# Two cross-attention layers on one core: ScalarE drains a slot's first unit ahead of the exponential and the copy of the maxima

## The chip, the cores and the metric

The kernel runs on one core of a Trainium2 chip. TensorE multiplies matrices into PSUM, ScalarE (ACT) and VectorE (DVE) work on PSUM and SBUF, GpSimd (POOL) works on SBUF and issues DMAs, SyncE (SP) issues DMAs. The metric is the device time of one execution in microseconds; of several executions the median is given.

## What is computed

For each of 16 batch entries a query matrix `x` of 112 rows and 320 columns passes through two cross-attention layers over the same context of 375 rows and 192 columns. Layer 0 has 8 heads of 40 columns over 371 context rows, and a second, small attention path over the last 4 rows, whose result is added before the output projection. Layer 1 has 20 heads of 16 columns over all 375 rows. Cut to what matters:

```python
# layer 0
hs = mha(x @ Wq, enc @ Wk, enc @ Wv)            # 8 heads, 371 keys
ca_hs1 = mha(ca_q1, x, x)                       # 112 x 112 scores for each head
ca_hs2 = mha(ca_hs1 @ Wq, ca @ Wk_ca, ca @ Wv_ca)   # 4 keys
x1 = (hs + ca_hs2) @ Wout + b_out + x
# layer 1
q, k, v = x1 @ Wq, ctx @ Wk, ctx @ Wv           # 20 heads, 375 keys
out = softmax(q k^T / 4) v @ Wo + bo + x1
```

## The kernel before

**Groups and slots.** The attention of both layers runs in groups of four heads: two groups of layer 0 and five of layer 1 for each batch entry. The main loop has 18 iterations (`t` from 0 to 17, `ITERATIONS`) of seven slots (`SLOTS`); each slot works on three groups at once, one in each stage:

- *scores*: TensorE computes the scores of a group in two halves into `bankS` (`scores`, L1120 for layer 0, L1124 for layer 1), and VectorE takes the row maxima of each half (L762);
- one slot later, *maxima*: TensorE transposes the maxima into `bankO` (`transpose_m`, L1137), VectorE copies them to `mT` (L768), and ScalarE issues a small DMA that places them as an additional row of the queries (`place_m`, L569 for layer 0, L572 for layer 1);
- two slots later (`LAG`), the *late* group: TensorE computes the transposed scores with the maxima already subtracted into `bankST` (`shifted_scores`, L1153 and L1166; this waits for the placed maxima), ScalarE takes the exponential (`exps`, L557 and L558 for layer 0, L561 for layer 1), and TensorE multiplies it with the values into `bankO` (`attend`, L1200; this waits for the exponential). VectorE copies the product (L779).

**Units.** All the rest (projections, transposes, the small attention path) is cut into 35 units for each batch entry. Each fills one of two PSUM banks (`bankX`), which alternate in the order of the units; a unit may be written only when the unit two before it is drained. The table `UNITS` gives for each slot two lists, phase 0 and phase 1, as names and offsets of the batch entry against `t`:

```python
([("W2", 1), ("V1_0", -1)], [("q1T_0", -1), ("V1_1", -1), ("q1T_1", -1)]),
([("V1_2", -1), ("q1T_2", -1), ("K1_0", 0)], [("N1a", -2), ("q0", 1), ("p3T", 0)]),
([("K1_1", 0), ("N1b", -2), ("S2_0", 1)], [("hn1T", -2), ("K1_2", 0), ("S2_1", 1)]),
([("K0_0", 1), ("q0T_0", 1)], [("K0_1", 1), ("out1", -2)]),
([("N0", 0), ("K0_2", 1), ("q0T_1", 1)], [("hn0T", 0), ("T2_0", 1), ("V0_0", 1)]),
([("T2_1", 1), ("out0", 0), ("V0_1", 1)], [("x1T", 0), ("PV2", 1)]),
([("q1", 0), ("S3", 1)], [("V0_2", 1)]),
```

`units_of(t, i, phase)` leaves out those whose batch entry doesn't exist, so in the first and last iterations a list may begin with another unit or be empty. K0, K1, V0, V1, q0, q1, out0 and out1 are projections (L968), five to nine matmuls each in split precision; q0T, q1T, hn0T, hn1T, x1T, T2, N0, N1a and N1b are transposes; W2, S2, PV2, S3 and p3T belong to the small path.

**The order on each engine** is written out by hand, and each engine works its program in order. TensorE in a slot: first half of the scores, transposed scores of the late group, transpose of the maxima, units of phase 0, second half of the scores, attend of the late group, units of phase 1. VectorE: maximum of the first half, copy of the transposed maxima, phase 0, maximum of the second half, copy of the attended product, phase 1. ScalarE, in the loop that the diff touches (L697 to L707): exponential of the late group, DMA of the maxima, phase 0, phase 1.

**Drains.** `unit` of ScalarE copies a filled bank to SBUF: K1 at L603, K0 at L609, V0 at L616, V1 at L624, q0 at L632, q1 at L637, q0T at L642, q1T at L648, W2 at L653, T2 at L655. For N0, N1a, N1b, out0 and out1 it returns at once, since VectorE alone drains these. For K0, K1, q0, q1 and W2 ScalarE writes the rounded part, and VectorE subtracts it afterwards to get the rest (L798 for K1, L803 for K0, L753 for q0, q1 and W2); only then is the bank free. S2 is drained by four exponentials (L579), after VectorE's maximum (L820).

Of the kernel before, what the change touches and what calls it, by code (L numbers as in the profile page):

```python
# [57 lines left out]
def units_of(t, i, phase):  # L58

    return [(name, t + off) for name, off in UNITS[i][phase]  # L60
            if 0 <= t + off < B and not (off == 1 and t < 0)]
# [30 lines left out]
def scored_at(t, i, before=0):  # L92

    n = SLOTS * t + i - before
    return SCORED.get((n // SLOTS, n % SLOTS))
# [22 lines left out]
def xattn_kernel(nc, xT, xpad, ctxT, caS, caT, w_all, w_ca, wqT, bd96, consts, bias, out):  # L118
    g_rows = nc.dram_tensor("g_rows", [B, 3, 32, HID], F32, kind="Internal").ap()

    with ExitStack() as ctx:
# [414 lines left out]
        def _(act):  # L536
# [12 lines left out]
            def exps(g):  # L549
                layer, b, k = g  # L550
                n = NUMBER[g]
                dst = PT[:, n % 2]
                act.wait_ge(st_done, n + 1)
                if n >= 2:
                    act.wait_ge(pv_done, n - 1)
                if layer == 0:
                    nc.scalar.activation(dst[0:KC, 0:2, :], bankST[0:KC, 0:2, 0:GROUP * SQ], ACT.Exp)  # L557
                    nc.scalar.activation(dst[0:KC - NTOK, 2, :], bankST[0:KC - NTOK, 2, 0:GROUP * SQ], ACT.Exp)\  # L558
                        .then_inc(exp_done, 1)
                else:  # L560
                    nc.scalar.activation(dst[0:KC], bankST[0:KC, :, 0:GROUP * SQ], ACT.Exp).then_inc(exp_done, 1)  # L561

            def place_m(g):
                layer, b, k = g
                n = NUMBER[g]
                src = mT[:, n % MT_BUFS, :].bitcast(F32)
                act.wait_ge(mT_copied, n + 1)
                if layer == 0:
                    act.dma_start(q0T[M_ROW0:M_ROW0 + 1, GROUP * k:GROUP * k + GROUP, :].bitcast(F32),  # L569
                                 src.unsqueeze(1)).then_inc(m0_placed, 16)  # L570
                else:
                    act.dma_start(q1T[b % 2][M_ROW1:M_ROW1 + 65:64, 2 * k:2 * k + 2, :].bitcast(F32),  # L572
                                 src).then_inc(m1_placed, 16)
# [93 lines left out]
            def round_p3(b):  # L667
                act.wait_ge(p3_ready, b + 1)
                src = p3[:, :, :].rearrange("p h n -> p (h n)").unsqueeze(1)
                nc.scalar.activation(p3w[:, 0:3:2, :].bitcast(F32R), src.broadcast_to((SQ, 2, H0 * NTOK)), ACT.Copy)\  # L670
                    .then_inc(p3_rounded, 1)
# [23 lines left out]

            for t in ITERATIONS:
                for i in range(SLOTS):  # L697
                    if scored_at(t, i, LAG):
                        exps(scored_at(t, i, LAG))
                    if scored_at(t, i, 1):  # L700
                        place_m(scored_at(t, i, 1))
                    for u in units_of(t, i, 0):
                        unit(*u)
                    for u in units_of(t, i, 1):
                        unit(*u)
                    if i == SLOTS - 1 and t + 1 < B:
                        round_p3(t + 1)  # L707

        @block.vector
        def _(dve):  # L710
# [79 lines left out]
            def unit(name, b):  # L790
                X = bankX[bank(name, b)]
                free = bank_drained[bank(name, b)]
                kind, _, i = name.partition("_")
                i = int(i or 0)
                if kind == "K1":
# [125 lines left out]
        def _(pe):  # L921
# [49 lines left out]
            def unit(name, b):  # L971
                X = bankX[bank(name, b)]
                kind, _, i = name.partition("_")
                i = int(i or 0)
                if AT[name, b] >= 2:
# [339 lines left out]
```

## Time and profile before

| | |
|---|---|
| median of three runs | 867.8 us (863.59 to 873.38) |
| profiled execution: time | 864.51 us |
| its span, first to last instruction | 862.7 us |
| TensorE busy | 756.3 us, 88% of the span |
| VectorE, ScalarE, GpSimd busy | 446.3, 403.7 and 297.2 us |
| mean granted TensorE clock | 0.942 |

Busy shares are means over the span, and matmuls are pipelined with modelled ends, so a busy TensorE is not one at its peak. Which engine holds which is read from the waits (what an engine stood idle for, and what ended it) and from the timeline (instructions in order of time). A slot takes some 5 to 10 us, an iteration about 47 us. The first iterations, up to about 130 us, and the last, from about 800 us, differ from the regular ones between them.

### The profile page before, as it was taken

How to read it: one execution, taken by the hardware profiler on the slowest of the kernel's cores; microseconds unless marked ns; L12 is line 12 of the kernel's file. 1: busy time of each engine (PE TensorE's matmuls, PEld its weight loads, DVE VectorE, ACT ScalarE, POOL GpSimd, SP SyncE). 2: the span in 40 equal slices, each digit the busy share in tenths (PEclk: the TensorE clock that was granted, in tenths of full speed). 3: DMA queues.
4: the chain of work that ended last, by engine and by line, in shares of the span. 5: the costliest groups of instructions: out<-in, count | busy, mean ns of one | idle time of the engine just before them, and what ended most of it. 6: DMA issues, size and time to landing. Idle time of an engine off the chain costs nothing.

```text
span 862.7 us, 19114 instructions
## 1 busy us (share of the span) xinstructions
PE 756.3 (88%) x7400; PEld 606.7 (70%) x7400; DVE 446.3 (52%) x979; ACT 403.7 (47%) x922; POOL 297.2 (34%) x410
## 2 busy tenths in 40 slices
PE   5981879999898999999998989999998999899886
PEld 4641667777777777777777778777776877777664
DVE  3530335555555555555655556565656465565452
ACT  3310435455555455554554554555555545554322
POOL 7224453423242525234232415252343324141100
PEclk9765999999999999999999999999999999999865
DMA  9313344334251615243342516162433334151300
GB/s 297 96 25 78 85 103 98 77 75 114 52 128 42 145 36 132 56 96 74 71 111 53 131 40 143 36 133 55 102 75 79 99 65 119 21 129 31 46 8 8
DMA packets 51895, 72.54 MB, mean 84 GB/s; under 512 B 12912, under 2 KB 43504, under 8 KB 51808
## 3 DMA queue, kind: packets, MB, share of 16 engines
q1 hardware_dynamic: 43200, 59.88, 28.8%
q0 software_dynamic: 7872, 11.24, 6.3%
q8 instruction: 61, 1.00, 0.5%
q10 hardware_dynamic: 736, 0.20, 0.1%
q14 instruction: 26, 0.21, 0.1%
HBM read 20.60 MB, written 4.26 MB: 29 GB/s over the span
## 4 chain that ended last, share of the span: by engine, by line
PE 65%; ACT 15%; DVE 7%; issue 3%; DMA 1%; ACTq 1%; POOL 0%
PE bankX L968 25%; PE bankO L1200 10%; PE bankST L1166 7%; PE bankS L1124 5%; ACT arena L579 4%; PE bankST L1153 3%; ACT arena L561 3%; PE bankS L1120 2%; ACT arena L557 2%; DVE stage L798 2%; PE bankX L1050 2%; DVE negmax L820 2%; PE bankX L1041 2%; PE bankX L1058 2%; ACT stage L603 2%
## 5 line engine op out<-in xcount | busy, mean ns | idle before, releaser
L762 DVE TENSOR_REDUCE negmax<-bankS 112x2 f32<-112x750 f32 (+1 forms) x224 | 208.3, 930 | 69.6 <-PE bankS L1120 34.5
L561 ACT ACTIVATE arena<-bankST 125x1344 f32<-125x1344 f32 x80 | 103.4, 1293 | 80.6 <-PE bankST L1166 80.6
L1200 PE MATMUL bankO<-arena,v 125*32 125x112 f32 (+2 forms) x2688 | 111.5, 272 | 10.1 <-ACT arena L558 5.3
L1200 PEld LDWEIGHTS bankO<-arena,v 125*32 125x32 f32 (+2 forms) x2688 | 84.1, 121 | 35.0 <-issue 17.9
L462 POOL TENSOR_TENSOR arena<-arena,rsum 112x896 f32<-112x896 f32 x16 | 26.9, 1684 | 233.8 <-DVE rsum L860 233.8
L490 POOL DMA_DIRECT2D k_stack<-stage x192 | 96.1, 508 | 26.0 <-DVE stage L798 24.9
L968 PE MATMUL bankX<-ctx_hi,WH 128*120 128x376 f32 (+2 forms) x192 | 74.3, 387 | 11.3 <-ACT v L624 9.4
L968 PE MATMUL bankX<-WH,ctx_hi 128*125 128x320 f32 x192 | 69.5, 362 | 14.3 <-DVE act_hi L849 13.7
L1166 PEld LDWEIGHTS bankST<-q1T,k_stack 49*125 49x125 f32 x960 | 68.4, 195 | 11.2 <-issue 7.0
L1166 PE MATMUL bankST<-q1T,k_stack 49*125 49x112 f32 x960 | 71.0, 280 | 2.7 <-DMA q1T<-mT 2.7
L1124 PE MATMUL bankS<-k_stack,q1T 48*112 48x376 f32 x320 | 70.0, 434 | 3.5 <-DVE negmax L762 3.4
L798 DVE TENSOR_TENSOR stage<-bankX,stage 128x376 fp32r<-128x376 f32 (+1 forms) x48 | 26.3, 547 | 77.4 <-ACT stage L603 77.4
L968 PE MATMUL bankX<-ctx_hi,WL 128*120 128x376 f32 (+2 forms) x192 | 65.1, 339 | 0.0
L579 ACT ACTIVATE arena<-bankX,negmax 112x112 f32<-112x112 f32 x128 | 43.5, 353 | 43.8 <-DVE negmax L820 43.8
L968 PE MATMUL bankX<-WL,ctx_hi 128*125 128x320 f32 x192 | 59.0, 315 | 0.0
L455 POOL TENSOR_TENSOR w2bd<-w2s,cst 96x896 fp32r<-96x896 f32 x16 | 26.9, 1680 | 88.2 <-DVE w2s L753 87.9
L803 DVE TENSOR_TENSOR stage<-bankX,stage 120x376 fp32r<-120x376 f32 (+1 forms) x48 | 26.3, 548 | 55.8 <-ACT stage L609 55.8
L968 PEld LDWEIGHTS bankX<-WH,ctx_hi 128*125 128x125 f32 x192 | 36.6, 191 | 25.7 <-DVE act_hi L849 17.0
L968 PEld LDWEIGHTS bankX<-ctx_hi,WH 128*120 128x120 f32 (+2 forms) x192 | 35.4, 185 | 21.0 <-ACT v L624 12.5
L968 PE MATMUL bankX<-WH,act_hi 128*112 128x320 f32 x144 | 48.4, 336 | 2.0 <-DVE act_hi L849 1.8
L1124 PEld LDWEIGHTS bankS<-k_stack,q1T 48*112 48x112 f32 x320 | 28.4, 174 | 30.9 <-issue 17.9
L1153 PE MATMUL bankST<-q0T,k_stack 121*125 121x112 f32 (+1 forms) x384 | 49.3, 279 | 0.0
(135 smaller groups left out, 1546.0 us busy)
## 6 DMA issues: line engine op xcount, KB each, us to landing
k_stack<-stage SPq DMA_DIRECT2D x96, 176.2 KB
k_stack<-stage SPq DMA_DIRECT2D x192, 70.5 KB, 2.6
k_stack<-stage POOLq DMA_DIRECT2D x192, 47.0 KB, 2.4
ctx_raw<-in_ctxT SPq DMA_DIRECT2D x16, 376.0 KB, 3.3
k_stack<-stage SPq DMA_DIRECT2D x48, 117.5 KB
xp<-in_xpad SPq DMA_DIRECT2D x16, 224.0 KB, 3.3
x_raw<-in_xT SPq DMA_DIRECT2D x16, 168.0 KB, 2.6
out<-x1b SPq DMA_DIRECT2D x16, 140.0 KB, 2.3
```

The lines of the kernel that those rows point to most:

```text
L455: nc.gpsimd.tensor_tensor(w2bd[:, :, :], w2s[:, :].bitcast(F32).unsqueeze(1).broadcast_to((96, H0, SQ)), mask96.unsqueeze(2).broadcast_to( ...
L462: nc.gpsimd.tensor_tensor(prob2[0:SQ], prob2[0:SQ], rsum2[:, :].unsqueeze(2).broadcast_to((SQ, H0, SQ)), ALU.mult).then_inc(prob2_ready, 1)
L490: pool.dma_start(dst, src).then_inc(k1_stacked_pool[b % 2], 16)
L561: nc.scalar.activation(dst[0:KC], bankST[0:KC, :, 0:GROUP * SQ], ACT.Exp).then_inc(exp_done, 1)
L579: last = nc.scalar.activation(prob2[0:SQ, h, :], X[0:SQ, (h % 4) * SQ:(h % 4 + 1) * SQ], ACT.Exp, bias=negmax2[:, h:h + 1], accum_out=sum2 ...
L762: nc.vector.tensor_reduce(negmax[:, n % 2, first:first + step + 1:step], bankS[0:SQ, :, 0:keys], axis=AX, op=ALU.max, negate=True).then_in ...
L798: nc.vector.tensor_tensor(k1_lo[0:rows, i, :].bitcast(F32R), X[0:rows, 0:SKP], k1_hi[0:rows, i, :], ALU.subtract).then_inc(free, 1)
L968: last = nc.tensor.matmul(dst, lhs, rhs, start=(n == 0), stop=(n == len(passes) - 1))
L1124: last = nc.tensor.matmul(bankS[0:SQ, j, 0:SKP], q1T[b % 2][row, h // 2, :], k1_stack[b % 2][row, h // 2, :], start=True, stop=True)
L1153: last = nc.tensor.matmul(bankST[0:keys, n_bank, col:col + SQ], k0_stack[0:M_ROW0 + 1, h, KC * c:KC * c + keys], q0T[0:M_ROW0 + 1, h, :], ...
L1166: last = nc.tensor.matmul(bankST[0:KC, n_bank, col:col + SQ], k1_stack[b % 2][row, h // 2, KC * c:KC * c + KC], q1T[b % 2][row, h // 2, :] ...
L1200: last = nc.tensor.matmul(dst, v, src[0:keys, n_bank, col:col + SQ], start=(c == 0), stop=(c == NKC - 1))
```

## The change

In ScalarE's loop the first unit of phase 0 is taken from the list and drained ahead of the exponential and of the DMA of the maxima; the others stay behind these. TensorE's and VectorE's programs are not touched, and SyncE's and GpSimd's neither.

```diff
             for t in ITERATIONS:
                 for i in range(SLOTS):
+                    first, *others = units_of(t, i, 0) or [None]
+                    if first:
+                        unit(*first)
                     if scored_at(t, i, LAG):
                         exps(scored_at(t, i, LAG))
                     if scored_at(t, i, 1):
                         place_m(scored_at(t, i, 1))
-                    for u in units_of(t, i, 0):
+                    for u in others:
                         unit(*u)
                     for u in units_of(t, i, 1):
                         unit(*u)
```

ScalarE's program at the start of slot 6 of a regular iteration and on into slot 0 of the next, before (`arena` holds the exponentials, `mT` the maxima, `qn` the drained q1, `w2s` the drained W2):

```order
L561 ACTIVATE arena<-bankST 125x1344
L572 DMA q1T<-mT 2x2x112
L637 ACTIVATE qn<-bankX 112x40x16
L595 ACTIVATE p<-p 112x32
L616 ACTIVATE v<-bankX 125x8x40
L670 ACTIVATE p3w<-p 112x2x32
L561 ACTIVATE arena<-bankST 125x1344
L572 DMA q1T<-mT 2x2x112
L653 ACTIVATE w2s<-bankX 96x112
L624 ACTIVATE v_1<-bankX 125x20x16
```

The same place of ScalarE's program after:

```order
L637 ACTIVATE qn<-bankX 112x40x16
L561 ACTIVATE arena<-bankST 125x1344
L572 DMA q1T<-mT 2x2x112
L595 ACTIVATE p<-p 112x32
L616 ACTIVATE v<-bankX 125x8x40
L670 ACTIVATE p3w<-p 112x2x32
L653 ACTIVATE w2s<-bankX 96x112
L561 ACTIVATE arena<-bankST 125x1344
L572 DMA q1T<-mT 2x2x112
L624 ACTIVATE v_1<-bankX 125x20x16
```

The drain of q1 (L637) and that of W2 (L653) each stand ahead of an exponential and its DMA now.

ScalarE's program from the start of slot 2 to the exponentials of slot 3, before (`stage` holds the drained keys; the exponentials here are of layer 0, in two instructions):

```order
L557 ACTIVATE arena<-bankST 125x896
L558 ACTIVATE arena<-bankST 121x448
L569 DMA q0T<-mT 1x4x112
L603 ACTIVATE stage<-bankX 128x376
L579 ACTIVATE arena,sum<-bankX,negmax 112x112 x4
L661 ACTIVATE act_hi<-bankX 128x224
L662 ACTIVATE act_hi<-bankX 64x112
L603 ACTIVATE stage<-bankX 64x376
L579 ACTIVATE arena,sum<-bankX,negmax 112x112 x4
L557 ACTIVATE arena<-bankST 125x896
L558 ACTIVATE arena<-bankST 121x448
L572 DMA q1T<-mT 2x2x112
```

The same stretch after:

```order
L603 ACTIVATE stage<-bankX 128x376
L557 ACTIVATE arena<-bankST 125x896
L558 ACTIVATE arena<-bankST 121x448
L569 DMA q0T<-mT 1x4x112
L579 ACTIVATE arena,sum<-bankX,negmax 112x112 x4
L661 ACTIVATE act_hi<-bankX 128x224
L662 ACTIVATE act_hi<-bankX 64x112
L603 ACTIVATE stage<-bankX 64x376
L579 ACTIVATE arena,sum<-bankX,negmax 112x112 x4
L609 ACTIVATE stage<-bankX 120x376
L557 ACTIVATE arena<-bankST 125x896
L558 ACTIVATE arena<-bankST 121x448
```

K1_1's drain (the first L603) and K0_0's (L609) stand ahead of the exponentials of slots 2 and 3.

## Rows read from the trace of the kernel before

**Rows 1.** The page, chain that ended last, shares of the span by engine

```profile
PE 65%; ACT 15%; DVE 7%; issue 3%; DMA 1%; ACTq 1%; POOL 0%
```

**Rows 2.** Waits of TensorE, 130 to 800 us: total, times, longest, in us

```profile
PE bankX L1075 <- DVE stage L798: 17.3, 13, 1.4
PE bankX L968 <- DVE act_hi L849: 12.8, 14, 0.9
PE bankX L968 <- ACT v L624: 8.1, 14, 0.6
PE bankO L1200 <- ACT arena L558: 4.6, 15, 0.8
```

**Rows 3.** Timeline, slot 6: start, duration (us), engine, line, operation [idle before <-releaser]

```profile
440.85 1.30 ACT L561 ACTIVATE arena<-bankST 125x1344 f32<-125x1344 f32 x1 [0.44 <-PE bankST L1166]
...
441.87 0.31 PE L968 MATMUL bankX<-WL,act_hi 128*112 128x320 f32 x1
...
442.21 0.70 ACT L637 ACTIVATE qn<-bankX 112x640 fp32r<-112x640 f32 x1
...
443.18 0.78 PE L1200 MATMUL bankO<-arena,v 125*32 125x112 f32 x24
```

**Rows 4.** Timeline, slot 0: W2's matmuls, W2's drain, the attend product

```profile
397.75 0.91 PE L1069 MATMUL bankX<-x_raw,bd 128*96 128x112 f32 x6
...
399.15 0.26 ACT L653 ACTIVATE w2s<-bankX 96x112 fp32r<-96x112 f32 x1
...
399.86 0.78 PE L1200 MATMUL bankO<-arena,v 125*32 125x112 f32 x24
```

**Rows 5.** Timeline, slot 3: K0_0's last matmul, the exponentials, K0_0's drain, the attend

```profile
231.96 0.33 PE L968 MATMUL bankX<-ctx_hi,WL 128*120 128x376 f32 x1
232.00 0.93 ACT L557 ACTIVATE arena<-bankST 125x896 f32<-125x896 f32 x1
...
232.79 0.56 ACT L558 ACTIVATE arena<-bankST 121x448 f32<-121x448 f32 x1
233.22 0.51 ACT L609 ACTIVATE stage<-bankX 120x376 fp32r<-120x376 f32 x1
233.41 1.38 PE L1200 MATMUL bankO<-arena,v 125*64 125x112 f32 x24 [0.28 <-ACT arena L558]
```

**Rows 6.** Timeline, slot 1: V1_2's last matmul and drain, K1_0's first matmul and drain

```profile
215.73 0.31 PE L968 MATMUL bankX<-WL,ctx_hi 128*125 128x320 f32 x1
...
216.32 0.43 ACT L624 ACTIVATE v<-bankX 125x320 f32<-125x320 f32 x1
...
216.81 0.44 PE L968 MATMUL bankX<-ctx_hi,WH 128*128 128x376 f32 x1 [0.58 <-ACT v L624]
...
217.97 0.48 ACT L603 ACTIVATE stage<-bankX 128x376 fp32r<-128x376 f32 x1 [0.97 <-PE bankX L968]
```

**Rows 7.** Timeline, slot 2: K1_1's last matmul and drain, the attend product

```profile
223.47 0.34 PE L968 MATMUL bankX<-ctx_hi,WL 128*128 128x376 f32 x1
...
224.10 0.49 ACT L603 ACTIVATE stage<-bankX 128x376 fp32r<-128x376 f32 x1
...
225.98 1.38 PE L1200 MATMUL bankO<-arena,v 125*64 125x112 f32 x24
```

**Rows 8.** Timeline, slot 0 of iteration 16: V1_0's last matmul, the attend product

```profile
816.89 0.31 PE L968 MATMUL bankX<-WL,ctx_hi 128*125 128x320 f32 x1
817.13 0.78 PE L1200 MATMUL bankO<-arena,v 125*32 125x112 f32 x24
```

**Rows 9.** Timeline: a DMA of the maxima issued, the transposed scores that waited for it

```profile
799.24 0.55 ACTq L572 DMA_DIRECT2D q1T<-mT  x1
...
804.20 1.50 PE L1166 MATMUL bankST<-q1T,k_stack 49*125 49x112 f32 x12 [2.57 <-DMA q1T<-mT]
```

**Rows 10.** Busy time in two iterations: length, PE, PEld, DVE, ACT, POOL, granted clock, DMA share, GB/s

```profile
213.69:260.83 47.14, 43.88 (x461) 35.49 (x459) 26.67 (x60) 24.67 (x58) 17.00 (x24) 1.00 0.37 86
402.19:450.54 48.35, 45.09 (x461) 36.97 (x459) 26.67 (x60) 24.69 (x58) 16.99 (x24) 0.96 0.37 84
```

## The prediction

> **What bounds the kernel now.** The chain that ended last comes first: 65% of the span is TensorE's and 15% ScalarE's [rows 1], so the question is where TensorE stands still. Its waits between 130 and 800 us, the thirteen to fourteen regular iterations, come next [rows 2]. Four places repeat once in an iteration: S2_0 waits 1.3 us for the drain of K1_1 (17.3 us in 13 times), V0_0 0.9 us for hn0T, K1_0 0.58 us for the drain of V1_2 (8.1 in 14), and the attend product of slot 3 0.3 us for the exponential (4.6 in 15). All the rest of an iteration TensorE runs through. Hence a later exponential costs time as soon as it ends after TensorE reaches the attend of that slot, and an earlier drain pays only in the places just named. So I replay each slot with the rows of the timeline that stand at its first unit.
>
> **The change part by part.** No instruction is added or removed: ScalarE runs the same 804 rows, and a drain of 0.26 to 0.70 us, with its wait for the filled bank, moves ahead of an exponential of 1.29 us (two of together about 1.4 us in layer 0) and the DMA of the maxima. VectorE's part of the drain follows ScalarE's. TensorE, VectorE, GpSimd and SyncE keep their order. The exponential was free to start when the transposed scores were done; now it also waits until TensorE has done the copy of the maxima's transpose and all the first unit, and until ScalarE has drained it. In slot 4 the first unit is N0, which ScalarE doesn't drain, so nothing moves there. Two overheads are read from rows: ScalarE takes up a filled bank about 0.04 us after the last matmul's end, and an ACTIVATE that is ready starts 0.1 us before the one ahead of it ends (232.79 against 232.00 + 0.93 [rows 5]; I use 0.09); the attend follows the exponential's end by 0.05 us.
>
> *Slot 6 (q1 first)* [rows 3]. q1's last matmul ends at 441.87 + 0.31 = 442.18. Now the exponential has run by then (440.85 to 442.15) and q1's drain starts at 442.21 anyway: moving it gains nothing. After the change the drain is at the same place, 442.21 to 442.91, the exponential 442.82 to 444.11, the attend at 444.16 instead of 443.18: **+0.98 us**. Iterations 1 to 15: 14.7 us.
>
> *Slot 0 (W2 first)* [rows 4]. W2 is full at 397.75 + 0.91 = 398.66, drained 398.70 to 398.96 (0.26); the exponential, 1.29 long, would run 398.90 to 400.19; the attend starts at 400.24 instead of 399.86: **+0.38**. V1_0's drain slips too, but its bank is next wanted only after the attend and q1T_0. Thirteen times (iterations 2 to 14): 4.9 us.
>
> *Slot 3 (K0_0 first)* [rows 5]. K0_0 is full at 231.96 + 0.33 = 232.29. The two exponentials begin now at 232.00 and the attend follows 1.41 us later, at 233.41. After: drain 232.33 to 232.84 (0.51), exponentials from 232.74, attend at 232.74 + 1.41 = 234.15: **+0.74**, on top of the 0.3 that is there. Fifteen times: 11.1 us.
>
> *Slot 1 (V1_2 first)* [rows 6]. V1_2 is full at 216.04 and drained 216.08 to 216.51, so K1_0 can start at 216.57 instead of 216.81; the exponential runs 216.43 to 217.72, and the attend, 0.9 us and more behind K1_0's start, finds it done. But the drains of q1T_2 and K1_0 now stand behind the later exponential. K1_0's starts at 217.97 in the row; after, not before 217.72 + 0.26 (the drain of q1T_2 is no shorter than W2's) less two overlaps, 217.80. VectorE's work on K1_0, a maximum and N1a follow it, and p3T waits for these. So between 0 and 0.17 arrives: I take **-0.1**, fourteen times, -1.4 us (-3.4 if nothing behind held it).
>
> *Slot 2 (K1_1 first)* [rows 7]. K1_1 is full at 223.47 + 0.34 = 223.81, so its drain starts at 223.85 instead of 224.10 and S2_0 follows **0.25** earlier. The drain gains no more, because it waits for its matmuls. The attend's earliest moment is 223.85 + 0.49 - 0.09 + 1.41 = 225.66, and TensorE comes to it at 225.98 - 0.25 = 225.73: covered, by 0.07. Fourteen times, -3.5 us. In iterations 0 and 1 N1b is missing, so that cover is gone: I price each like slot 3, +0.74, together 1.5.
>
> *Slot 5 (T2_1 first).* V0_1 takes T2_1's bank, but no wait of V0_1's matmuls stands among the waits [rows 2], so an earlier drain gains 0; the exponential has the nine matmuls of out0 and the five of V0_1 as cover. 0.
>
> *Iterations 15 and 16.* W2 is missing, so V1_0 is the first unit of slot 0, and there is little behind it on TensorE: the attend comes at 817.13 [rows 8], while V1_0 is full at 817.20; drain 817.24 to 817.68, exponential to 818.88, attend at 818.93, +1.8 us. Two such slots 0 and one slot 1: 5.4 us.
>
> Sum: 14.7 + 4.9 + 11.1 - 1.4 - 3.5 + 1.5 + 5.4 = 32.7 us. The profiled execution took 864.5 us (a span of 862.7 and 1.8 around it): 864.5 + 32.7 = **897 us**. It lies 3.3 below the median of 867.8 of the three runs shown, which reach from 863.6 to 873.4; on the median the sum would be 900.5.
>
> **Does ScalarE really stand still at the first unit?** The forecast rests on it. The Trainium skill (TensorE: Matmul & The Clock Gate, section "Architectural detail: the array is 16× 32×32, not 1× 128×128") says that ScalarE's queue is strictly first in, first out. It speaks against this change, since whatever is ready behind a waiting drain waits too; no row here shows that directly.
>
> **The rivals.**
>
> *Faster: the exponential stays covered.* If ScalarE could start the exponential before the waiting unit, or TensorE had enough work ahead of the attend, only the gains would stay: K1_0 with its full 0.24 and S2_0 with 0.25, each 14 times: 6.9 us, that is 858 us. It decides at the work between the end of the transposed scores and the attend: slot 6 would need 1.37 + 0.70 + 1.29, about 3.3 us (q1's end is 1.37 behind the scores' end, which is 0.04 ahead of 440.85), and has 443.18 - 440.81 = 2.4 [rows 3]. Chance 4%.
>
> *No change: something else already holds the attend.* The attend also waits for the maxima's copy and the product before. If these ended as late as the new exponential, slots 3 and 6 would cost nothing: 897.2 - 25.8 = 871 us. VectorE ends the last of these before the attend in every slot above, and in slot 3 the exponential is named as the releaser. Chance 5%.
>
> *The maxima come too late.* Their DMA is issued behind the exponential. In the worst case shown it was issued at 799.24 and TensorE went on at 804.20, 5.0 us later, with a wait of 2.57 [rows 9]. In slot 6 the issue moves by about a microsecond, but so does the next slot that needs it. In slot 5 the issue moves by at most 0.6 us (mostly T2_1's drain) and its user does not move; at 0.6 in all 14 iterations that is 8.4 us more, 906 us. Chance 5%, and nothing in the sum.
>
> *The clock.* An iteration in which the granted clock stayed at full speed took 47.14 us, one with a mean of 0.96 took 48.35 [rows 10]: a drop to the lower level (1.2 instead of 2.4 GHz) costs 1.2 us. In that iteration it followed the 1.3 us wait of S2_0. That wait gets shorter, while two of about 1 us arise in every iteration (slot 3 with 0.3 + 0.74, slot 6 with 0.98). The 0.9 us wait in slot 4 is as long and there already. If every second new wait brought a drop, 15 drops would cost 18 us: 915 us; if a few do, 2 to 6 us. The Trainium skill (TensorE: Matmul & The Clock Gate, "A second HAM failure mode: psum-queue depth-cycling") says that frequent short idles between groups of matmuls make the clock swing between its levels. By that the second half of this rival would hold; in the rows most of the iterations with such waits keep the full clock. Chance of more than 10 us: 8%.
>
> **How the numbers follow.** The forecast, a loss of 20 to 45 us, has 78%; the clock 8, the late maxima 5, no change 5, faster 4. Its own range is made by the terms: slot 1 between 0 and -2.4, slot 0 between 0.2 and 0.5 each time (2.6 to 6.5, since ends of matmuls are modelled), slot 3 up to 0.9 (13.5), iterations 0, 1, 15 and 16 between half and all: together 890 to 903, to which come the 3.3 us of the median and a few drops of the clock. The range 885 to 910 takes in these and the late maxima, and leaves out both cases below and the worst of the clock. About 1% is what a measurement of this kernel can tell from no change: slower by over 1% gets 78 + 8 + 5 = 91%, within 1% 5%, faster 4%.
>
> **What would show it.** In the profile of the changed kernel busy times stay as they are, and TensorE's waits at the attend product for the exponential grow from some 5 us to about 35, in slots 0, 3 and 6; the wait of K1_0 for V1_2's drain falls to about 0.35 us each and that of S2_0 to about 1.05. ScalarE's exponential of layer 1 waits no longer for the transposed scores in slot 6, but starts straight behind q1's drain. I am wrong if the attends don't wait, if waits for the maxima's DMA appear at the transposed scores, or if the mean granted clock leaves 0.94 by more than 0.02.

## The result, and the profile after

The changed kernel takes 900.0 us (median of four runs, 897.2 to 901.6) where the kernel before takes 865.7 (four runs, 862.7 to 873.4): a ratio of 1.038, 95% interval 1.034 to 1.043, so 33 us slower. The profiled execution of the changed kernel took 897.2 us, 32.7 more than that of the kernel before.

In the profile's page TensorE's busy time grew by 8.0 us (from 756.3), and in the chain that ended last its share fell from 65 to 60% [rows 1]: most of the time added is standing time.

```profile
PE 764.3 (85%) x7400; PEld 614.3 (69%) x7400; DVE 448.7 (50%) x979; ACT 395.8 (44%) x922; POOL 297.2 (33%) x410
...
PE 60%; ACT 13%; DVE 9%; issue 4%; ACTq 4%; DMA 0%; POOL 0%
```

TensorE's waits between 130 and 800 us (total, times, longest) answer to [rows 2]. The lines of the changed kernel behind the edit lie three further down (the attend product is L1203, the projections L971).

```profile
PE bankO L1203 <- ACT arena L561: 16.0, 27, 0.9
PE bankO L1203 <- ACT arena L558: 14.8, 15, 1.3
PE bankX L1078 <- DVE stage L801: 13.6, 13, 1.0
PE bankX L971 <- DVE act_hi L852: 12.8, 14, 0.9
PE bankX L971 <- ACT v L624: 4.7, 14, 0.3
```

The attend product now waits 30.8 us for its exponential, where it waited 4.6. S2_0's wait for K1_1's drain fell from 17.3 to 13.6 us, 0.28 each time, and K1_0's for V1_2's drain from 8.1 to 4.7, 0.24 each time. The wait for hn0T, which the change doesn't reach, stayed at 12.8.

The timeline of slot 6 (start, duration, engine, line, operation, idle time before and what ended it) answers to [rows 3]:

```profile
453.46 0.80 PE L1169 MATMUL bankST<-q1T,k_stack 49*125 49x112 f32 x12
...
454.52 0.25 DVE L771 CAST mT<-bankO 4x112 fp32r<-4x112 f32 x1
...
455.32 0.31 PE L971 MATMUL bankX<-WL,act_hi 128*112 128x320 f32 x1
...
455.67 0.70 ACT L637 ACTIVATE qn<-bankX 112x640 fp32r<-112x640 f32 x1 [1.81 <-PE bankX L971]
...
455.76 0.52 ACTq L572 DMA_DIRECT2D q1T<-mT  x1
...
456.27 1.28 ACT L561 ACTIVATE arena<-bankST 125x1344 f32<-125x1344 f32 x1
...
457.61 0.78 PE L1203 MATMUL bankO<-arena,v 125*32 125x112 f32 x24 [0.90 <-ACT arena L561]
```

ScalarE stands 1.81 us for q1's matmuls, the last 1.41 of them with the transposed scores done (453.46 + 0.80 = 454.26). It drains, and only then takes the exponential, straight behind the drain; the attend starts 1.98 us behind q1's end (455.63), where it started 1.00 behind it before. The row of the DMA is worth a look: the DMA of the maxima stands behind the exponential in the program, and its issue begins at 455.76, before the exponential runs. It doesn't wait for the end of the ACTIVATEs ahead of it, so the later exponential did not hold it. The drain's wait did: VectorE's copy of the maxima ends at 454.77, and the issue follows 0.99 us later, when q1 is full. In the kernel before it followed the copy by 0.03 us:

```profile
441.07 0.25 DVE L768 CAST mT<-bankO 4x112 fp32r<-4x112 f32 x1
...
441.35 0.52 ACTq L572 DMA_DIRECT2D q1T<-mT  x1
```

No matmul waits for this DMA between 130 and 800 us (one weight load does, for 0.2 us), so the maxima had that much to spare.

In slot 3 [rows 5]:

```profile
434.62 0.34 PE L971 MATMUL bankX<-ctx_hi,WL 128*120 128x376 f32 x1
...
434.99 0.48 ACT L609 ACTIVATE stage<-bankX 120x376 fp32r<-120x376 f32 x1 [0.21 <-PE bankX L971]
...
435.37 0.91 ACT L557 ACTIVATE arena<-bankST 125x896 f32<-125x896 f32 x1
...
436.77 1.38 PE L1203 MATMUL bankO<-arena,v 125*64 125x112 f32 x24 [0.99 <-ACT arena L558]
```

And TensorE's waits in slots 0, 1 and 2, which answer to [rows 4], [rows 6] and [rows 7]:

```profile
414.44 0.78 PE L1203 MATMUL bankO<-arena,v 125*32 125x112 f32 x24 [0.26 <-ACT arena L561]
...
419.64 0.44 PE L971 MATMUL bankX<-ctx_hi,WH 128*128 128x376 f32 x1 [0.33 <-ACT v L624]
...
427.90 0.45 PE L1078 MATMUL bankX<-w2bd,ca_st 96*112 96x448 f32 x1 [1.05 <-DVE stage L801]
```

**Slot by slot.** I set the start of every slot's scores beside its start in the kernel before; what a slot adds to this lag is its price. In the regular iterations the prices repeat to 0.02 us, apart from slots 2 and 3 of iterations 2 and 7, where the clock fell in the kernel before, and slot 6 of iterations 3 and 4 (+1.21 and +0.88):

| slot (unit moved) | predicted | measured |
|---|---|---|
| 0 (W2) | +0.38 | +0.31 |
| 1 (V1_2) | -0.10 | -0.14 |
| 2 (K1_1) | -0.25 | -0.27 |
| 3 (K0_0) | +0.74 | +0.70 |
| 4 (N0, nothing moves) | 0 | 0.00 |
| 5 (T2_1) | 0 | -0.17 |
| 6 (q1) | +0.98 | +0.97 |
| an iteration | +1.75 | +1.40 |

Iterations 2 to 14 together: 13 × 1.40 = 18.2 us. The granted clock fell twice in this stretch of the kernel before and not in the changed one, which gives back about 2.4 (1.2 each, [rows 10]). Of the rest of the 32.7, 16.9 us by this sum and 16.6 by the lags, 3.8 come in iterations 0 and 1 and 8.4 from iteration 15 on. The other 4.3 stand there already at the first scores of the loop. Ahead of these the order is the same in all kernels of this document, and the same lag lies between -3.0 and +7.4 us in the others: it is chance of the start. The trace of the kernel before had a fast one. Its iteration 2 begins at 159.8 us; in the traces of `regular`, `early125`, `late036` and `tail` below, whose order up to there is the same, it begins at 164.5 to 165.5, in the changed kernel at 167.9.

### The profile page after: what moved, and what is told of

The parts are those of the page before. It is cut to its first block, busy times and chain, and to the rows that moved or that the text cites. A ratio compares the mean times of both kernels' runs of the same rounds, so it can differ in the third digit from the quotient of the medians.

```text
span 895.4 us, 19114 instructions
## 1 busy us (share of the span) xinstructions
PE 764.3 (85%) x7400; PEld 614.3 (69%) x7400; DVE 448.7 (50%) x979; ACT 395.8 (44%) x922; POOL 297.2 (33%) x410
## 4 chain that ended last, share of the span: by engine, by line
PE 60%; ACT 13%; DVE 9%; issue 4%; ACTq 4%; DMA 0%; POOL 0%
PE bankX L971 22%; PE bankO L1203 9%; PE bankST L1169 7%; PE bankST L1156 5%; ACT arena L561 5%; PE bankS L1127 4%; ACTq L572 3%; ACT arena L579 2%; PE bankX L1044 2%; DVE stage L801 2%; PE bankO L1140 2%; PE bankX L1053 2%; DVE negmax L765 2%; ACT stage L603 2%; PE bankX L1092 1%
## 5 line engine op out<-in xcount | busy, mean ns | idle before, releaser
L1203 PE MATMUL bankO<-arena,v 125*32 125x112 f32 (+2 forms) x2688 | 113.2, 275 | 46.2 <-ACT arena L561 26.7
L1203 PEld LDWEIGHTS bankO<-arena,v 125*32 125x32 f32 (+2 forms) x2688 | 85.4, 122 | 73.1 <-ACT arena L561 41.0
L971 PE MATMUL bankX<-ctx_hi,WH 128*120 128x376 f32 (+2 forms) x192 | 74.4, 387 | 8.4 <-ACT v L624 5.0
L971 PE MATMUL bankX<-WH,ctx_hi 128*125 128x320 f32 x192 | 69.2, 360 | 14.3 <-DVE act_hi L852 13.7
L971 PE MATMUL bankX<-ctx_hi,WL 128*120 128x376 f32 (+2 forms) x192 | 65.6, 342 | 0.0
L971 PE MATMUL bankX<-WL,ctx_hi 128*125 128x320 f32 x192 | 60.4, 321 | 0.0
L971 PEld LDWEIGHTS bankX<-WH,ctx_hi 128*125 128x125 f32 x192 | 37.4, 195 | 22.7 <-DVE act_hi L852 17.0
L971 PE MATMUL bankX<-WH,act_hi 128*112 128x320 f32 x144 | 48.8, 339 | 1.8 <-DVE act_hi L852 1.8
L1156 PEld LDWEIGHTS bankST<-q0T,k_stack 121*125 121x125 f32 (+1 forms) x384 | 44.8, 190 | 5.6 <-issue 5.5
```

Source lines behind the costliest of these rows:

```text
L971: last = nc.tensor.matmul(dst, lhs, rhs, start=(n == 0), stop=(n == len(passes) - 1))
L1156: last = nc.tensor.matmul(bankST[0:keys, n_bank, col:col + SQ], k0_stack[0:M_ROW0 + 1, h, KC * c:KC * c + keys], q0T[0:M_ROW0 + 1, h, :], ...
L1203: last = nc.tensor.matmul(dst, v, src[0:keys, n_bank, col:col + SQ], start=(c == 0), stop=(c == NKC - 1))
```

## The experiments

All kernels below are the kernel before with another order in ScalarE's loop. The first diff is against the kernel before; a diff that only replaces a line with `ahead` is against `regular`, where it isn't said otherwise. Gains and losses in us are the ratio times the median of the kernel before in the same comparison (867 to 868 us).

### Which iterations: the regular ones, the ends

```diff
+                    ahead = 1 if 2 <= t <= 14 else 0
+                    for u in units_of(t, i, 0)[:ahead]:
+                        unit(*u)
                     if scored_at(t, i, LAG):
                         exps(scored_at(t, i, LAG))
                     if scored_at(t, i, 1):
                         place_m(scored_at(t, i, 1))
-                    for u in units_of(t, i, 0):
+                    for u in units_of(t, i, 0)[ahead:]:
                         unit(*u)
```

This is `regular`; it does the change in iterations 2 to 14.

> First unit ahead in all slots, iterations 2 to 14 alone. Theory A: the steps add up, 1.98 - 0.58 = 1.40 us an iteration, 18.2 us: about 884 us, and the time of this run minus the time before is the sum of those of the two halves within 3 us. Rival B or C, where a wait in one slot feeds another: not the sum.

885.2 us, ratio 1.023 (1.017 to 1.028), 20 us. The slots' prices are those of the table. Its complement does the change in the other four iterations:

```diff
-                    ahead = 1 if 2 <= t <= 14 else 0
+                    ahead = 0 if 2 <= t <= 14 else 1
```

> First unit ahead in iterations 0, 1, 15 and 16 alone, where units are missing and less work covers the exponential. Theory A by the two traces: what is left of the whole loss, 34.3 - 18.2 = 16 us: about 882 us. By the prediction's own terms: 1.5 + 5.4 and one each of slots 3 and 6, about 10 us: 876 us. If the first lag of 4.3 us in the trace, which lies ahead of the loop, is chance: 877 to 878 us.

885.6 us, ratio 1.023 (1.017 to 1.028), again 20 us. That is twice the prediction's terms for these iterations, 10.0. Of the 21.9 us that its trace is longer than that of the kernel before, 3.8 stand ahead of the loop, 8.4 come in iterations 0 and 1 and 9.2 from iteration 15 on. So I took the ends apart, first `t <= 1` and then `t >= 15`:

```diff
-                    ahead = 1 if 2 <= t <= 14 else 0
+                    ahead = 1 if t <= 1 else 0
```

> The first unit ahead in iterations 0 and 1 alone. The run with the ends alone took 18.7 us, and its trace puts about 10 of them into iterations 15 and 16 and only 1 to 3 into those steps of iterations 0 and 1 where an attend product waits for its exponential. Theory A, the steps of the trace are the whole price: the rest of that run's loss was the clock's chance, and this kernel takes 868 to 870 us where the kernel before takes 867. Theory B, the two first iterations cost what is left of the 18.7, 8 us: 875.

873.4 us, ratio 1.007 (1.002 to 1.012): 6.0 us, from 1.7 to 10.2. This lies between both theories and decides for neither. The first iterations can't be read from a single pair of traces either: with their order untouched, slot 0 of iteration 1 started at 117.1 us in the kernel before, and at 120.4, 121.8 and 122.8 in three of the kernels here (`tail`, `regular`, `early125`). What the trace of this kernel adds inside iteration 1 (+1.1 in slot 0, -0.9 in slot 1, +0.6 in slot 2, +0.9 in slot 3, -0.2 in slot 5, +1.0 in slot 6) comes to 2.4 us; slot 0's +1.1 is chance, since `tail`, unchanged there, has +1.2. Iteration 2 begins at 168.4 us here, 2.9 to 3.9 behind the four kernels with the old order up to there. The prediction had 3.9 for iterations 0 and 1, well inside the interval.

```diff
-                    ahead = 1 if 2 <= t <= 14 else 0
+                    ahead = 1 if t >= 15 else 0
```

> The first unit ahead in iterations 15 and 16 alone. By the steps in the trace of the kernel with the ends alone, 10.3 us: 877 us where the kernel before takes 867. By the terms of the prediction (5.4 for V1_0 in three slots, 0.98 and 0.74 for slots 6 and 3, 0.25 back in slot 2, about 6.9): 874. If the slot 2 in which the products of S2 are missing has no cover, the attend product there waits about 1.35 us for the exponential.

A ratio of 1.011 (1.006 to 1.015), 9.3 us, from 5.4 to 13.2; by the lags of its trace 10.3. (The expectation's 6.9 for the prediction's terms is 0.7 too high: iteration 15 has no K0_0 in slot 3, and the prediction hadn't counted one. It had 6.1.) Head and tail together make 15.3, between the 12.2 that the changed kernel's profile shows for these iterations and the 20 of `ends`, at the lower edge of its interval (15 to 24). TensorE's rows of `tail` show where the price lies: slots 0, 2 and 6 of iteration 15, and slots 0 and 1 of iteration 16.

```profile
781.30 0.78 PE L1203 MATMUL bankO<-arena,v 125*32 125x112 f32 x24 [1.37 <-ACT arena L561]
...
794.38 1.38 PE L1203 MATMUL bankO<-arena,v 125*64 125x112 f32 x24 [1.36 <-ACT arena L558]
...
821.08 0.78 PE L1203 MATMUL bankO<-arena,v 125*32 125x112 f32 x24 [1.62 <-ACT arena L561]
...
825.70 1.35 PE L1203 MATMUL bankO<-arena,v 125*32 125x112 f32 x24 [1.71 <-ACT arena L561]
...
833.52 1.35 PE L1203 MATMUL bankO<-arena,v 125*32 125x112 f32 x24 [1.51 <-ACT arena L561]
```

In a regular slot 2 the exponentials are covered by S2_0, in slot 6 by S3 as well as q1. Both units belong to the next batch entry and don't exist in iteration 15, so TensorE reaches the attend sooner and waits 1.36 and 1.62 us, where the regular slots wait 0 and 0.90.

### Which slots: the late ones, the early ones

`late036` does the change in slots 0, 3 and 6 of the regular iterations, `early125` in slots 1, 2 and 5:

```diff
-                    ahead = 1 if 2 <= t <= 14 else 0
+                    ahead = 1 if i in (0, 3, 6) and 2 <= t <= 14 else 0
```

> First unit ahead in slots 0, 3 and 6 alone, iterations 2 to 14. Theory A (the exponential ends late at the attend): the three lags seen between the two traces, 0.31 + 0.70 + 0.97 = 1.98 us an iteration, 13 times, 25.7 us: about 891 us, slower by 3.0%. Rival B (the copied maxima come late): most of the loss would belong to slots 1, 2 and 5 as much as to these, about 878 us. Rival C (the clock, drawn down by waits anywhere): a loss that is not 13 equal steps but a few of 1.2 us or more, with a mean granted clock below 0.93.

894.6 us, ratio 1.035 (1.029 to 1.041), 30 us, from 25 to 36. The steps of its trace, +0.31, +0.70 and +0.97 and all others 0.00, make 25.7 in thirteen iterations, at the lower edge. TensorE's waits between 130 and 830 us: the attend's for the exponential are there in full, and K1_1's drain holds TensorE as before (so does V1_2's):

```profile
PE bankX L1078 <- DVE stage L801: 17.3, 13, 1.4
PE bankO L1203 <- ACT arena L561: 15.5, 27, 0.9
PE bankO L1203 <- ACT arena L558: 13.5, 15, 1.0
```

```diff
-                    ahead = 1 if 2 <= t <= 14 else 0
+                    ahead = 1 if i in (1, 2, 5) and 2 <= t <= 14 else 0
```

> First unit ahead in slots 1, 2 and 5 alone, iterations 2 to 14. Theory A: there the exponential stays covered and only the earlier drains count, -0.14 - 0.27 - 0.17 = -0.58 us an iteration, 13 times, -7.5 us: about 858 us, faster by 0.9%. Rival B (late maxima): slot 5 hands its maxima over with the least to spare, so waits at the transposed scores of slot 6 take the gain back: 862 to 870 us. Rival C (clock): the wait of S2_0 falls from 1.3 to 1.05 us, fewer drops, up to 2.4 us more gain: 856 us.

860.6 us, ratio 0.992 (0.988 to 0.996): faster than both kernels, by 6.8 us (3.4 to 10) against the kernel before (by its steps, -0.14, -0.26 and -0.17, 7.4). TensorE's waits between 130 and 830 us:

```profile
PE bankX L1078 <- DVE stage L801: 13.6, 13, 1.1
...
PE bankX L971 <- ACT v L624: 6.2, 15, 1.3
PE bankO L1203 <- ACT arena L558: 4.8, 15, 0.8
```

The same move is worth 7 us in three slots and costs 30 in three others. Slot 5's -0.17 was not in my sum. It was there to be read, among the waits of the weight loads (PEld) of the kernel before, which I hadn't asked for:

```profile
PEld bankX L968 <- ACT arena L655: 2.8, 14, 0.2
```

V0_1's first weight load stood 0.2 us for T2_1's drain in each of 14 iterations. In the changed kernel the row is gone.

### A larger dose: two units ahead

If the price is the time from the attend's arrival to the end of the exponential, it must grow with the work put ahead. `slot4_two` takes two units ahead in slot 4, where the first (N0) is no work for ScalarE and the second is K0_2; `slot6_two` takes q1 and S3 ahead in slot 6. Nothing else moves in them.

```diff
-                    ahead = 1 if 2 <= t <= 14 else 0
+                    ahead = 2 if i == 4 else 0
```

> Slot 4 alone, where the change moved nothing: N0 (no work for ScalarE) and K0_2 ahead of the exponential. Theory A, by the same working from rows of the kernel before: K0_2 is full at 428.87 + 0.33 = 429.20, drain 429.24 to 429.72, exponential 429.63 to 430.92, attend at 430.97 instead of 430.07: +0.90 us, in iterations 1 to 14 12.6 us: about 879 us, slower by 1.45%. If the loss of the change had to do with which units are first, and not with when the exponential ends: no change, 867 us.

891.7 us, ratio 1.022 (1.014 to 1.030), 19 us. The step in slot 4 is +0.89, as worked out, where the clock doesn't fall, or 12 us in thirteen iterations. The rest is the granted clock, which fell in five of them, with no longer single wait than the kernel before has. One such stretch (length, PE, PEld, DVE, ACT, POOL, granted clock, DMA share, GB/s):

```profile
290.50:304.20 13.70, 11.97 (x97) 10.09 (x97) 6.09 (x13) 5.18 (x9) 6.72 (x13) 0.75 0.63 154
```

```diff
-                    ahead = 1 if 2 <= t <= 14 else 0
+                    ahead = 2 if i == 6 else 0
```

> Slot 6 alone, with q1 and S3 ahead of the exponential: the same cause with a larger size. Theory A: S3's exponential starts at 443.80, when VectorE has made its input; the large one follows at 443.95 to 445.24, the attend at 445.29 instead of 443.18: +2.1 us, 14 times, and in iteration 15, where S3 is missing, about 1.9: 31 us, about 898 us, slower by 3.6%. Rival C (the clock): waits of 2 us on TensorE bring a drop to the lower level in most iterations, 5 to 17 us more.

929.1 us, ratio 1.069 (1.064 to 1.073), 59 us, twice what theory A gave. Its step is right, +2.08 where the clock doesn't fall within the slot, 27 us in thirteen iterations. But the clock falls in most of them: by the lags these iterations add 56 us, so the rival that I priced at 5 to 17 us takes 29. The attend's wait, among TensorE's waits between 130 and 830 us:

```profile
PE bankO L1203 <- ACT arena L561: 26.1, 13, 2.0
```

And the granted clock of three stretches (same columns): one right behind such a wait of 2.00 us, the full clock again, and one that begins behind the next such wait:

```profile
576.90:580.90 4.00, 3.97 (x40) 3.19 (x41) 1.34 (x6) 0.58 (x2) 0.00 (x0) 0.57 0.00 0
580.90:625.00 44.10, 40.83 (x420) 33.13 (x418) 23.88 (x51) 22.10 (x53) 17.01 (x24) 1.00 0.38 86
...
628.40:635.20 6.80, 6.80 (x32) 5.80 (x33) 2.33 (x8) 2.13 (x4) 0.94 (x1) 0.50 0.07 18
```

### The DMA of the maxima

The change moves a unit past the exponential and past the DMA of the maxima. `exp_first` moves it past the DMA alone: exponential, first unit, DMA. Its diff and the next are against the kernel before.

```diff
+                    ahead = 1
                     if scored_at(t, i, LAG):
                         exps(scored_at(t, i, LAG))
+                    for u in units_of(t, i, 0)[:ahead]:
+                        unit(*u)
                     if scored_at(t, i, 1):
                         place_m(scored_at(t, i, 1))
-                    for u in units_of(t, i, 0):
+                    for u in units_of(t, i, 0)[ahead:]:
                         unit(*u)
```

> The exponential first, then the first unit's drain, then the DMA of the maxima: the unit overtakes the DMA alone. Theory A: the drains stand in time where they stood, the DMA leaves up to about 2 us later and is still in time in nearly all slots: 865 to 869 us, within 0.5% of before. Rival B: waits at the transposed scores, above all in slots 5 and 6, where the placed maxima had 0.1 to 1.6 us to spare: 875 us or more.

866.2 us, ratio 0.997 (0.994 to 1.001): no difference. The maxima are not what the change pays for.

`maxima_first` puts the DMA ahead of the first unit and of the exponential:

```diff
+                    ahead = 1
+                    if scored_at(t, i, 1):
+                        place_m(scored_at(t, i, 1))
+                    for u in units_of(t, i, 0)[:ahead]:
+                        unit(*u)
                     if scored_at(t, i, LAG):
                         exps(scored_at(t, i, LAG))
-                    if scored_at(t, i, 1):
-                        place_m(scored_at(t, i, 1))
-                    for u in units_of(t, i, 0):
+                    for u in units_of(t, i, 0)[ahead:]:
                         unit(*u)
```

> The DMA of the maxima first, then the first unit's drain, then the exponential: the unit overtakes the exponential alone. Theory A (the late exponential is the whole loss): as the changed kernel, 899 to 902 us, slower by 3.8%; holding the exponential for the maxima's copy adds nothing, since that copy ends before the first unit is drained. Rival B (the late maxima carry a part): that part comes back, 885 to 895 us.

931.2 us, ratio 1.072 (1.066 to 1.078), 62 us: both theories were wrong. Earlier maxima win nothing, and the DMA holds everything behind it. Slot 4 shows it alone, since its first unit is no work for ScalarE:

```profile
454.77 0.55 ACTq L572 DMA_DIRECT2D q1T<-mT  x1
455.43 1.29 ACT L561 ACTIVATE arena<-bankST 125x1344 f32<-125x1344 f32 x1 [2.88 <-DVE mT L771]
```

The exponential starts 0.66 us behind the start of a DMA that itself waited for VectorE's copy of the maxima, and the wait of ScalarE is put down to that copy (L771), which the exponential doesn't need. In the changed kernel slot 4 costs nothing, here 0.47 us in every iteration.

To see the DMA's part without the unit's, `dma_first` leaves the units where they were (DMA, exponential, units). Against `maxima_first`:

```diff
-                    ahead = 1
+                    ahead = 0
```

> No unit moves; the DMA of the maxima stands ahead of the exponential. Theory A: ScalarE's queue stands at the DMA until VectorE has copied the maxima, and for 0.65 us of issue. From the rows of the kernel before, the exponential then starts 0.59 us later in slot 3 and 1.05 to 1.2 later in slots 1, 2, 4, 5 and 6, and the drains behind it as well; V1_2's, K1_1's and T2_1's drains hold TensorE by 1.14, 1.05 and 1.17, the attend products of slots 0, 3, 4 and 6 by 0.2, 0.59, 0.47 and 0.16: 4.8 us in an iteration, with the first and last iterations about 85 us together: 930 to 960 us, slower than with the first unit ahead too (931). Theory B, the costs of the DMA and of the unit simply add: the steps of that kernel less those of the change, 1.27 us in an iteration and 29 us in all: 895.

1003.9 us, ratio 1.156 (1.148 to 1.163), 135 us: the costs don't add, and the direction of theory A is right, but the time lies 44 us above its range. ScalarE in slots 1 and 2:

```profile
407.25 0.65 ACTq L569 DMA_DIRECT2D q0T<-mT  x1
408.00 1.29 ACT L561 ACTIVATE arena<-bankST 125x1344 f32<-125x1344 f32 x1 [1.87 <-DVE mT L771]
409.19 0.43 ACT L624 ACTIVATE v<-bankX 125x320 f32<-125x320 f32 x1
...
416.12 0.61 ACTq L569 DMA_DIRECT2D q0T<-mT  x1
416.83 0.92 ACT L557 ACTIVATE arena<-bankST 125x896 f32<-125x896 f32 x1 [2.35 <-DVE mT L771]
...
418.07 0.49 ACT L603 ACTIVATE stage<-bankX 128x376 fp32r<-128x376 f32 x1
```

V1_2's and K1_1's drains stand behind DMA and exponential, and TensorE waits for them:

```profile
409.67 0.44 PE L971 MATMUL bankX<-ctx_hi,WH 128*128 128x376 f32 x1 [1.81 <-ACT v L624]
...
419.19 0.71 PE L1078 MATMUL bankX<-w2bd,ca_st 96*112 96x448 f32 x1 [2.42 <-DVE stage L801]
```

The granted clock up to slot 2 and in slot 2 (same columns as above):

```profile
405.30:413.80 8.50, 6.69 (x69) 5.38 (x67) 3.35 (x7) 3.30 (x7) 3.42 (x3) 1.00 0.16 47
413.80:425.46 11.66, 9.24 (x58) 7.30 (x57) 5.04 (x11) 4.51 (x16) 0.00 (x0) 0.71 0.03 11
```

K1_0 waits 1.81 instead of 0.58 and S2_0 2.42 instead of 1.3, 1.23 and 1.1 longer (1.14 and 1.05 expected); T2_1's step is +1.12 (1.17 expected), slots 3 and 4 come to about 0.5 each as expected. Slots 0 and 6 I had put too low (+0.71 and +0.87 against 0.2 and 0.16). The largest miss is the clock: the stretch with S2_0's wait was granted 0.71 on the mean, and the steps of slots 1 and 2 together lie between 3.7 and 5.8 us in the regular iterations, where 2.2 was expected.

The difference of the last two kernels is the change's own move, first unit ahead of the exponential, and here it makes the kernel 73 us *faster* (1004 to 931). With the DMA in front, the drains of V1_2, K1_1 and T2_1 are what TensorE waits for longest, and moving them up shortens that. A part of the 73 is the clock (mean 0.879 against 0.920 in the profiles).

A DMA stops ScalarE when it stands first, and issues beside running ACTIVATEs when it stands behind. `exp_first` shows one thing more: behind an ACTIVATE that still waits for its input, the DMA waits too. Slot 1 of `exp_first`, in the order exponential, V1_2's drain, DMA:

```profile
410.13 0.26 DVE L771 CAST mT<-bankO 4x112 fp32r<-4x112 f32 x1
...
410.53 0.31 PE L971 MATMUL bankX<-WL,ctx_hi 128*125 128x320 f32 x1
...
410.89 0.65 ACTq L569 DMA_DIRECT2D q0T<-mT  x1
...
411.13 0.43 ACT L624 ACTIVATE v<-bankX 125x320 f32<-125x320 f32 x1
```

The maxima are copied at 410.39 and V1_2 is full at 410.84. The DMA is issued at 410.89: not 0.03 us behind the copy, as in every slot of the kernel before, but as soon as the drain has its input, and before the drain runs. The Trainium skill (Perfetto Trace Analysis, section "Per-engine timelines") draws the semaphore wait of an ACTIVATE in a wait queue, with the sequencer already free for the next instruction. By that the DMA would not wait for the drain's bank; these rows, and the 0.99 us in slot 6 of the changed kernel, show that here it does.

## Why the prediction was right

**The mechanism** was the one predicted: ScalarE does not start an exponential that is ready while the drain ahead of it waits. In slot 6 it stands 1.81 us, 1.41 of them with the transposed scores done. Each of the steps in slots 0 to 4 and 6 came within 0.07 us of its working, so replaying a slot from rows, with a take-up of 0.04 us and an overlap of 0.1 between ACTIVATEs, is good enough to price such a move.

**The total** (897 us forecast, 900.0 measured as the median, 897.2 in the profile) was hit so closely by luck. In the profiles the sum of 32.7 was met exactly, but it was made of 22.7 for the regular iterations and 10.0 for the ends. Measured were 18.2 less about 2.4 for the clock, 12.2 in the first two and last two iterations, and 4.3 of chance ahead of the loop.

- *Regular iterations, 4.5 us too much.* Half of it is slot 5, set at 0 because "no wait of V0_1's matmuls stands among the waits". The wait stood among the weight loads; `early125` has the gain without the losses. Slots 0, 1, 2 and 3 each came out 0.02 to 0.07 below the working, together 0.17 an iteration. In slot 0 the exponential began 0.10 us before the end of W2's drain, and I had let it begin 0.06 before.
- *The ends, 2 to 5 us too little* (12.2 by the lags of the changed kernel, 15.3 by `head` and `tail`). Slots 2 and 6 were priced like regular ones in iteration 15, though S2_0 and S3 are missing there. I had looked for missing units at the front of a list (W2) and for one that serves as cover (N1b), and not for these two. Their attends wait 1.36 us where -0.25 was counted, and 1.62 where 0.98 was. That is 2.2 us more; the three slots with V1_0's terms came out somewhat lower (waits of 1.37, 1.71 and 1.51 against 1.8 each), and a lower clock at the end adds to it (from iteration 15 on 0.71 on the mean in `tail` and in the changed kernel, 0.76 before). For the head, 6.0 us with an interval from 1.7 to 10.2 against 3.9, what is price and what is chance stays open: iteration 2 begins 2.4 to 3.9 us behind the kernels with the old order in the changed kernel and in `head`, but 6.5 or more in `ends`, whose order up to there is the same as theirs.

**The rivals.** *Faster* fell, but its core is true for three slots: `early125`. *Something else holds the attend* fell: the releaser is the exponential in slots 0, 3 and 6. *The maxima too late* fell with `exp_first`, and since no matmul waits for their DMA between 130 and 800 us, though its issue moved by about 1 us in slot 6. *The clock* did not take part in the steady stretch of the changed kernel, nor did the mean clock leave 0.94 by more than 0.02 (0.938 in the profile, 0.926 and 0.927 in the other runs). The iteration of the kernel before in which it fell [rows 10], up to S2_0's wait and behind it:

```profile
402.19:414.60 12.41, 10.51 (x95) 8.28 (x95) 6.18 (x14) 5.71 (x11) 3.42 (x3) 1.00 0.14 43
414.60:418.00 3.40, 3.40 (x29) 3.11 (x30) 1.49 (x3) 1.71 (x10) 0.00 (x0) 0.50 0.00 0
```

The changed kernel from 130 us on:

```profile
130.00:480.00 350.00, 314.89 (x3267) 255.14 (x3266) 194.33 (x430) 174.11 (x416) 122.48 (x171) 1.00 0.36 83
```

The kernel before has two such falls between 130 and 800 us, both behind S2_0's wait of 1.3 us. The changed kernel has none, with four waits of 0.9 to 1.05 us in every iteration; `regular` and `early125`, where S2_0 waits 1.05 too, have none in their changed iterations either. So the shorter wait of S2_0 seems to win back those 2.4 us, which the prediction did not count; it isn't shown, since `tail`, where S2_0 still waits 1.3 us, has no such fall and `head` and `late036` have one. The Trainium skill (TensorE: Matmul & The Clock Gate, "A second HAM failure mode: psum-queue depth-cycling") would have the frequent short idles make the clock swing. The changed kernel shows that four of them in an iteration need not; the kernels with waits of about 2 us (`slot6_two`, `dma_first`), and `slot4_two`, show the swing.

## What to carry to other kernels

Moving a drain ahead of other work on its engine wins only where the next user of its bank waits, and costs wherever the work behind it has less cover than the drain and the wait for its filling take; so decide slot by slot (here slots 1, 2 and 5: 0.8% faster than before) and not for the whole loop. Before pricing a repeated slot, check for the first and last iterations whether the units that serve as *cover* exist, not only those that move, and read the waits of the weight loads beside those of the matmuls. A DMA issue that has to wait is best kept behind all that is ready on its engine's queue, and it waits with an ACTIVATE ahead of it that isn't ready.

## What the runs showed of the hardware

- A wait of TensorE has a second price where the granted clock falls to its lower level behind it. With waits of 1.8 to 2.4 us once or twice in an iteration it fell in most iterations (`slot6_two`: mean clock 0.897; `dma_first`: 0.879); with one of 1.3 us in none to two of thirteen (`tail` none, `head` one, the kernel before two); with four of 0.9 to 1.05 us (the changed kernel) in none. In `slot4_two` it fell five times with waits of 1.3, 0.9 and 0.8 us, so the longest wait alone does not decide it; what does stays open.
- The issue of a small DMA takes ScalarE's queue 0.5 to 0.66 us. Behind ACTIVATEs that run this costs nothing, since it runs beside them; ahead of them it is paid in full, and the wait of the DMA too (135 us in `dma_first`, the falls of the clock among them). Behind an ACTIVATE that waits for its input the DMA waits as long (0.99 us behind the copy of the maxima instead of 0.03 in slot 6 of the changed kernel), and doesn't wait for it to run.
